# A GCN recommender on one core: the last bias spread by TensorE, two branches turned, constant products between gathers

## The reference

```python
def gcn_conv(x, W, b, src, dst, n):
    h = x @ W
    loops = jnp.arange(n, dtype=src.dtype)
    s, d = jnp.concatenate([src, loops]), jnp.concatenate([dst, loops])
    deg = jax.ops.segment_sum(ones, d, num_segments=n)
    dis = jnp.where(deg > 0, jax.lax.rsqrt(jnp.maximum(deg, 1e-12)), 0.0)
    msgs = h[s] * (dis[s] * dis[d])[:, None]
    return jax.ops.segment_sum(msgs, d, num_segments=n) + b

user_vec = user_emb[user_idx]                                 # 512 x 32
g = jax.nn.relu(gcn_conv(service_emb, W1, b1, src, dst, 6250))
g = gcn_conv(g, W2, b2, src, dst, 6250)
ctx = g[context_idx].reshape(512, 96)
x = jnp.concatenate([user_vec, ctx], axis=1)                  # 512 x 128
return x @ fc_W + fc_b                                        # 512 x 6250
```

## Time and profile before

| | us |
|---|---|
| median of 3 runs | 757.84 |
| their range | 755.71 to 758.91 |
| the profiled execution's own time | 756.2 |
| its span (first to last instruction) | 754.4 |
| TensorE busy | 598.7 (79%) |
| VectorE busy | 599.4 (79%) |
| ScalarE busy | 423.0 (56%) |
| GpSimd busy | 180.4 (24%) |
| granted clock of TensorE, mean | 0.891 of full speed |

### The profile page before, as it was taken

How to read it: one execution, slowest core, us unless ns; L and a number is a source line. 1 busy time by engine, 2 the same in 40 slices (tenths; PEclk the granted TensorE clock), 3 DMA queues, 4 the chain that set the end, 5 groups by cost and what they waited for, 6 DMA issues and landing times.

```text
span 754.4 us, 22006 instructions
## 1 busy us (share of the span) xinstructions
PE 598.7 (79%) x9516; PEld 562.5 (75%) x9516; DVE 599.4 (79%) x1436; ACT 423.0 (56%) x769; POOL 180.4 (24%) x181
## 2 busy tenths in 40 slices
PE   0443657657558665488989999999999999999797
PEld 0343557657558665478989999999999999999443
DVE  9999999999999999888999999999994211111486
ACT  4997089788888511246888888888877100000000
POOL 1100000020000000377777666666200000000600
PEclk9957679699687875588999999999999999999899
DMA  8000000000000000234655565556200799999386
GB/s 130 2 1 1 1 1 1 1 4 3 0 4 2 1 1 1 59 94 136 208 194 192 197 211 205 198 192 211 69 3 2 250 373 359 373 336 289 66 342 284
DMA packets 55337, 94.22 MB, mean 125 GB/s; under 512 B 20954, under 2 KB 42132, under 8 KB 55237
## 3 DMA queue, kind: packets, MB, share of 16 engines
q1 hardware_dynamic: 40532, 74.35, 27.8%
q0 software_dynamic: 5216, 9.91, 6.1%
q10 hardware_dynamic: 9488, 8.52, 3.5%
HBM read 48.53 MB, written 44.21 MB: 123 GB/s over the span
## 4 chain that ended last, share of the span: by engine, by line
PE 49%; DVE 41%; ACT 3%; DMA 2%; issue 2%; POOL 2%; SPq 0%; DVEq 0%; POOLq 0%
PE pp L1482 16%; PE pp L1500 14%; DVE arena L984 13%; DVE arena L985 12%; PE psY L1500 12%; PE pp L1601 6%; DVE arena L971 3%; DVE arena L1162 2%; ACT arena L732 2%; POOL arena L675 1%; PE pp L1418 1%; DMA arena<-ordered_keys,window 1%; DVE arena L979 1%; DVE arena L1149 1%; DVE arena L980 1%
## 5 line engine op out<-in xcount | busy, mean ns | idle before, releaser
L675 POOL DMA_INDIRECT arena<-ordered_keys,window x147 | 159.2, 1083 | 211.6 <-DMA ordered_keys<-arena 147.5
L812 ACT ACTIVATE arena<-pp 128x512 uint16<-128x512 f32 x308 | 171.9, 585 | 47.0 <-PE pp L1482 44.9
L1482 PE MATMUL pp<-arena 128*128 128x128 fp8e4 (+1 forms) x2401 | 188.7, 220 | 7.4 <-DVE arena L1163 7.4
L732 ACT ACTIVATE arena<-arena,neg_word 128x780 fp8e4<-128x780 bf16 (+1 forms) x200 | 170.2, 946 | 0.0
L1482 PEld LDWEIGHTS pp<-arena 128*128 128x128 fp8e4 (+1 forms) x2401 | 147.9, 98 | 8.2 <-issue 5.3
L1500 PE MATMUL psY<-arena 128*128 128x96 bf16 x2401 | 149.9, 206 | 0.5 <-ACT arena L812 0.4
L1500 PEld LDWEIGHTS psY<-arena 128*128 128x128 fp8e4 x2401 | 122.4, 97 | 1.4 <-ACT arena L812 0.7
L1162 DVE TENSOR_SCALAR arena<-arena 128x384 int32<-128x384 int32 (+7 forms) x224 | 110.2, 493 | 7.2 <-PE pp L1482 7.0
L984 DVE TENSOR_TENSOR arena<-arena 128x832 f32<-128x832 f32 (+4 forms) x121 | 107.4, 888 | 3.9 <-ACT arena L755 1.1
L985 DVE TENSOR_TENSOR arena<-arena 128x832 f32<-128x832 f32 (+4 forms) x121 | 106.9, 884 | 0.0
L1500 PE MATMUL pp<-arena 128*128 128x96 bf16 x2401 | 102.4, 206 | 0.6 <-issue 0.6
(11 more groups left out here) (205 smaller groups left out, 520.9 us busy)
## 6 DMA issues: line engine op xcount, KB each, us to landing
arena<-adjacency_spill SPq DMA_DIRECT2D x120, 196.0 KB, 4.1
adjacency_spill<-arena SPq DMA_DIRECT2D x21, 768.0 KB
out_dram<-arena SPq DMA_DIRECT2D x12, 512.0 KB, 2.8
adjacency_spill<-arena SPq DMA_DIRECT2D x7, 832.0 KB
arena<-adjacency_spill SPq DMA_DIRECT2D x22, 197.5 KB, 4.0
out_dram<-arena ACTq DMA_DIRECT2D x8, 512.0 KB, 2.9
arena<-in_L_rec_fc_b_dram SPq DMA_DIRECT2D x7, 392.0 KB, 8.5
adjacency_spill<-arena SPq DMA_DIRECT2D x4, 640.0 KB
```

Source lines behind the costliest of these rows:

```text
L675: nc.gpsimd.indirect_dma_start(gath[:, k, q, :], None, ordered, bass.IndirectOffsetOnAxis(ap=window[:, q, d:d + 1], axis=0)).then_inc(gat[ ...
L732: ins = nc.scalar.activation(cols8[n % BUFS][:, 4 * u:4 * u + 4, 0:c1 - c0], high4[:, :, c0:c1], ACT.Sign, bias=neg_word[:, u:u + 1], satu ...
L812: nc.scalar.mul(adj16[g % SLOTS][:, m0 * P:m1 * P], bank(gp)[:, 0:(m1 - m0) * P], PAIR_SCALE).then_inc(evicted, 1)
L1482: ins = MM(bank(gp)[:, (n - n0) // 2 * P:((n - n0) // 2 + 1) * P], src_hot(h, n - a), dst_hot(h, n - a), start=n % 2 == 0, stop=n % 2 == 1 ...
```

## The change

`fc_b` is no longer spread by the DMA. SyncE loads its 6250 numbers as 13 rows of up to 512 (12x512 and 1x106), three times over, into partitions 0 to 12, 32 to 44 and 64 to 76 of a cleared tile `b_rows`; they lie in space that the one-hot codes no longer need. VectorE does the clearing and then `spread_bias` once, at the end of group 12's turn (`g == NG - 2`): it turns the three copies into the upper, middle and lower bf16 part of the numbers (`b_parts`), and makes 13 matrices `b_pick` of 96x128 that pick one row of each third. After the second layer TensorE multiplies `b_pick[n]` with `b_parts`, thirteen products of 128x512 whose every row is the bias of those 512 columns, and VectorE (even n) and ScalarE (odd n) copy them to SBUF as `fcb`.

The products of constants: 4 in place of 36 behind the second layer, 3 behind the bias, and 4 behind each of the first two gathers of b = 0, which get a semaphore each (`first_rows`).

On VectorE and ScalarE `If(is_bad == 0)` with the usual path first becomes `If(is_bad == 1)` with the general path first. On TensorE and SyncE the order stays.

```diff
--- before.py
+++ after.py
@@ -91,7 +91,8 @@
 FIRST_FETCHES = {3: 3, 4: 16, 5: 28}
 LAG = 3
 SPILL_PARTS = 4
-RUN_UP = (8, 12, 36)
+RUN_UP = (8, 12, 4, 3)
+BETWEEN_ROWS = 4
 AHEAD_OF = {1: 12, 2: 12}
 LOADS_A_CHUNK = 4
 FC_PART = 784
@@ -404,6 +405,12 @@
         featT = at(E0 + 4 * RES_B, BATCH * 4, F32)
         xt = at(E0 + 4 * RES_B + BATCH * 4, 4 * GC * D * 4, F32).rearrange("p (k h f) -> p k h f", k=4, f=D)
 
+        b_rows = at(E0, BANK * 4, F32)
+        b_parts, b_mid = (at(E0 + BANK * 4 + k * BANK * 2, BANK * 2, BF16) for k in range(2))
+        b_of = at(E0 + 2 * BANK * 4, 64, F32)[:, 0:len(NCH)]
+        b_pick = at(E0 + 2 * BANK * 4 + 64, len(NCH) * P * 2, BF16).rearrange("p (n m) -> p n m", m=P)
+        assert 2 * BANK * 4 + 64 + len(NCH) * P * 2 <= 4 * RES_B and len(NCH) <= 32
+
         pp = [ctx.enter_context(nc.psum_tensor(f"pp{k}", [P, 2 * BANK], F32)) for k in range(3)]
         psY = ctx.enter_context(nc.psum_tensor("psY", [P, BANK], F32))
         psX = ctx.enter_context(nc.psum_tensor("psX", [P, BANK], F32))
...
+        first_rows = [sem(f"first_rows{c}") for c in range(CTX)]
+        b_zero, b_in, b_split, b_mm, psum_free = map(sem, ("b_zero", "b_in", "b_split", "b_mm", "psum_free"))
+        b_set = [sem(f"b_set{k}") for k in range(2)]
...
@@ -533,6 +543,8 @@
             w = min(SUBC, T - s * SUBC)
             eng.dma_start(ordered[s * SPAN:s * SPAN + w * P, :].rearrange("(j q t) o -> q j (t o)", q=P, t=P),
                           rows[:, s * SUBC // P:(s * SUBC + w) // P, :]).then_inc(ordered_out[WRITTEN[s]], 16)
+
+        fcW, fcb = (at(adj_at[place2[(NG + k) % 5]], N * 4, F32) for k in range(2))
 
         def write_out(eng, mine):
             out_v = out.rearrange("(p b) n -> p b n", b=BB)
@@ -590,21 +602,22 @@
                     c, e = (min(n * PAIR // 2 * 2 * P, bytes_of(g)) for n in (a, b))
                     sp.wait_ge(evicted, pairs_before(g) + b)
                     sp.dma_start(spill[g, :, c:e], at(adj_at[g % SLOTS] + c, e - c, U8)).then_inc(spilled[g % SLOTS], 16)
+            sp.wait_ge(b_zero, 1)
+            full = N // BANK
+            for k in range(3):
+                sp.dma_start(b_rows[32 * k:32 * k + full, :], fc_b[0:full * BANK].rearrange("(c n) -> c n", n=BANK)).then_inc(b_in, 16)
+                sp.dma_start(b_rows[32 * k + full:32 * k + full + 1, 0:N - full * BANK], fc_b[None, full * BANK:N]).then_inc(b_in, 16)
             for k in range(SLOTS):
                 sp.wait_ge(spilled[k], 16 * SPILL_PARTS * len(range(k, NSPILL, SLOTS)))
             sp.wait_ge(bad_set, 1)
             is_bad = nc.sync.value_load(bad[:], min_val=0, max_val=1)
 
-            def load_fc(slot, what):
+            def load_fc(slot):
                 tile = at(adj_at[slot], N * 4, F32)
-                whole = fc_W if what == 0 else fc_b[None, :].to_broadcast((P, N))
                 for c in range(0, N, FC_PART):
                     w = min(FC_PART, N - c)
-                    if what == 0:
-                        sp.dma_start(tile[0:CTX * D, c:c + w], whole[D:P, c:c + w]).then_inc(fc_in, 16)
-                        sp.dma_start(tile[CTX * D:P, c:c + w], whole[0:D, c:c + w]).then_inc(fc_in, 16)
-                    else:
-                        sp.dma_start(tile[:, c:c + w], whole[:, c:c + w]).then_inc(fc_in, 16)
+                    sp.dma_start(tile[0:CTX * D, c:c + w], fc_W[D:P, c:c + w]).then_inc(fc_in, 16)
+                    sp.dma_start(tile[CTX * D:P, c:c + w], fc_W[0:D, c:c + w]).then_inc(fc_in, 16)
 
             with sp.If(is_bad == 0):
                 sp.wait_ge(filled, pairs_before(NG))
@@ -615,9 +628,8 @@
                     for c in range(0, loads_of(ORDER[i]) * part, part):
                         w = min(part, bytes_of(ORDER[i]) - c)
                         sp.dma_start(at(adj_at[place2[i]] + c, w, U8), spill[ORDER[i], :, c:c + w]).then_inc(loaded[place2[i]], 16)
-                for k in range(2):
-                    sp.wait_ge(y2_done, NG - 4 + k)
-                    load_fc(place2[(NG + k) % 5], k)
+                sp.wait_ge(y2_done, NG - 4)
+                load_fc(place2[NG % 5])
             with sp.Else():
                 sp.wait_ge(g_set, 1)
                 for row, tile in ((1, g_int[0]), (0, g_src)):
...
@@ -694,7 +705,7 @@
             for b in range(BB):
                 for c in range(CTX):
                     nc.gpsimd.indirect_dma_start(feat[:, b, D * c:D * (c + 1)], None, table,
-                        bass.IndirectOffsetOnAxis(ap=ccl[:, b * CTX + c:b * CTX + c + 1], axis=0)).then_inc(rows_in[b], 16)
+                        bass.IndirectOffsetOnAxis(ap=ccl[:, b * CTX + c:b * CTX + c + 1], axis=0)).then_inc(rows_in[b] if b else first_rows[c], 16)
 
         @block.scalar
         def _(act):
@@ -824,10 +835,7 @@
                 c = first_chunk(g)
                 act.dma_start(table[c * P:(c + w) * P, :].rearrange("(h l) f -> l h f", l=P), xt[:, i % 4, 0:w, :]).then_inc(table_out[i % 4], 16)
 
-            with act.If(is_bad == 0):
-                for i, g in enumerate(ORDER):
-                    write_table(i, g)
-            with act.Else():
+            with act.If(is_bad == 1):
                 for layer in range(2):
                     act.wait_ge(g_table, 16 * (layer + 1))
                     with act.Fori(0, TURNS_G) as i:
@@ -835,6 +843,13 @@
                         nc.scalar.copy(g_stage, g_src[:, bass.ds(i * U, U)]).then_inc(g_staged, 1)
                 for g in range(NG):
                     write_table(g, g)
+            with act.Else():
+                for i, g in enumerate(ORDER):
+                    write_table(i, g)
+            for n, (c, w) in enumerate(NCH):
+                if n % 2 == 1:
+                    act.wait_ge(b_mm, n + 1)
+                    nc.scalar.copy(fcb[:, c:c + w], bank(n)[:, 0:w]).then_inc(b_set[1], 1)
             write_out(act, 1)
 
         @block.vector
@@ -1204,6 +1219,18 @@
                 link(V.tensor_reduce(worst[:], flag_row, axis=AX.X, op=ALU.max))
                 V.tensor_scalar(bad[:], worst[:], 0.0, None, ALU.is_gt).then_inc(bad_set, 1)
 
+            def spread_bias():
+                dve.wait_ge(b_in, 96)
+                link(V.tensor_copy(b_parts[:, :], b_rows[:, :]))
+                link(V.tensor_tensor(b_rows[:, :], b_rows[:, :], b_parts[:, :], ALU.subtract))
+                link(V.tensor_copy(b_mid[:, :], b_rows[:, :]))
+                V.tensor_copy(b_parts[32:64, :], b_mid[32:64, :])
+                link(V.tensor_tensor(b_rows[:, :], b_rows[:, :], b_mid[:, :], ALU.subtract))
+                V.tensor_copy(b_parts[64:96, :], b_rows[64:96, :])
+                link(V.tensor_tensor(b_of, ident[:, 0:len(NCH)], ident[:, 32:32 + len(NCH)], ALU.add))
+                link(V.tensor_tensor(b_of, b_of, ident[:, 64:64 + len(NCH)], ALU.add))
+                V.tensor_copy(b_pick[:, :, :], b_of.rearrange("p (n o) -> p n o", o=1).to_broadcast((P, len(NCH), P))).then_inc(b_split, 1)
+
             group_masks(0)
             group_fields(0)
             one_hots(0, 0)
@@ -1256,6 +1283,9 @@
                 if g + 2 < NG:
                     group_fields(g + 2)
                 post_sum(g)
+                if g == NG - 2:
+                    V.memset(b_rows[:, :], 0.0).then_inc(b_zero, 1)
+                    spread_bias()
             post_split(NG - 1)
             is_bad = nc.vector.value_load(bad[:], min_val=0, max_val=1)
 
@@ -1263,17 +1293,7 @@
 
                 V.tensor_tensor(x, x, dis_w(first_chunk(g), chunks_of(g)), ALU.mult).then_inc(table_ready, 1)
 
-            with dve.If(is_bad == 0):
-                for i, g in enumerate(ORDER):
...
-                    to_table(g, x)
-            with dve.Else():
+            with dve.If(is_bad == 1):
                 V.memset(g_zero, 0.0)
...
+            with dve.Else():
+                for i, g in enumerate(ORDER):
...
+                    to_table(g, x)
+
+            V.memset(b_of[:, 0:1], 0.0).then_inc(psum_free, 1)
+            for n, (c, w) in enumerate(NCH):
+                if n % 2 == 0:
+                    dve.wait_ge(b_mm, n + 1)
+                    V.tensor_copy(fcb[:, c:c + w], bank(n)[:, 0:w]).then_inc(b_set[0], 1)
 
             def copy_features(b):
                 dve.wait_ge(feat_T, b + 1)
@@ -1341,7 +1375,8 @@
                 V.tensor_scalar(featT[0:CTX * D, b * P:(b + 1) * P], psX[0:CTX * D, b % 2 * P:(b % 2 + 1) * P], bias2[:, 0:1], None, ALU.add).then_inc(feat_ready, 1)
             copy_features(0)
             mix_features(0)
-            dve.wait_ge(fc_in, 48 * -(-N // FC_PART))
+            for k in range(2):
+                dve.wait_ge(b_set[k], len(range(k, len(NCH), 2)))
             n = 0
             for b in range(BB):
                 for c, w in NCH:
@@ -1574,10 +1609,19 @@
                         ins = MM(ps[k][:, 0:w * D], g_zero[:, 0:P], g_zero[:, 0:w * D], start=False, stop=True)
                     ins.then_inc(g_summed, 1)
 
```

(20 more changed lines are left out.)

18 lines of the change are left out of this document (8 added, 10 removed).

## The result

The changed kernel takes 753.71 us in the median of 20 runs (750.75 to 759.55), the kernel before 757.7 us in 20 runs (754.74 to 761.18). The ratio is 0.995, 95% interval 0.9934 to 0.9966: 3.8 us faster, between 2.6 and 5.0. That is just at the bound of 0.5% that I had set. In two further sets of runs the same code stood at 0.996 (0.9941 to 0.998) and 0.9942 (0.9912 to 0.9973); one execution in the last, of 764.78 us, was in a slower state and stands outside that ratio. The forecast of 752.3 us was right in sign and 1.4 us too low; the range held the time.

The account below looks back on a forecast made before the run. The prediction took the chain through TensorE's second layer, then the last table write, gathers and output products, as the bound. Write -2.7 and clock -2.0 sum to -4.7 us, from 757.0 to 752.3 us; range 750.2 to 756.4.

Parts of the forecast that it names:

- Write of the table: Last write of `context_table`: without the spread load's traffic it takes 2.0 us instead of 4.7, -2.7 us.
- Preparing on VectorE: VectorE's preparing of the bias rows at group 12: at most 13.3 us, covered by idle time of 13.15 us, 0 us.
- Spreading: Thirteen bias products and their copies behind the second layer: done by 698.8, ahead of the transpose at 700.8, 0 us.
- Products by gather: Products of constants between the gathers keep TensorE's clock up for transpose and output and delay nothing: -2.0 us.
- Order of the branches: Jumps of VectorE and ScalarE moved ahead of the second layer: copies start at once, nothing else gained, 0 us.
- my start of 757.0: Whole kernel's starting time for the forecast: the middle of the profiled execution's 756.2 us and the runs' median, 757.84.
- Rival 1: TensorE's clock falls between the gathers, features come 1.2 us late: -2.5 us in all, 754.5 us; chance 0.23.
- Rival 3: Thirteen bias products each wait for a copy, end at 710 and hold the output by 4.6 us: about 761; chance 0.05.

Follow-up runs that it names:

- after: The first profile of the changed kernel, unaltered: the profiled execution took 754.08 us, with a span of 752.3.
- e9: Changed kernel with bias products ahead of TensorE's jump, 12 products of constants behind them, 4 and 1 between the gathers: 754.39 us, ratio 0.994 to the kernel before.
- e10: Changed kernel with only the bias products moved ahead of TensorE's jump, products of constants unaltered: 755.7 us, ratio 0.9956 to the kernel before.
- e11: The changed kernel once more, unaltered, in the last set, as a third profile: 755.44 us, ratio 0.9942 to the kernel before.
- e7: Changed kernel plus the spread load of fc_b as before, into a slot that nobody reads: 757.79 us, ratio 0.9997 to the kernel before.
- e3: Kernel before without the spread load of fc_b, nothing in its place: 756.92 us, ratio 0.9975 to the kernel before.
- e2: Changed kernel with the order of the branches on VectorE and ScalarE as before: 753.78 us, ratio 0.9955 to the kernel before.
- e1: Changed kernel with no products of constants between the gathers: 755.13 us, ratio 0.9967 to the kernel before.
- e6: Changed kernel with 4 products of constants behind the first gather and 1 behind the second: 753.37 us, ratio 0.9949 to the kernel before.
- e5: Changed kernel with TensorE's branch turned too, general path first: 762.79 us, ratio 1.0062 to the kernel before.
- e4: Kernel before with only 4 products of constants added behind each of the first two gathers, spread load kept: 757.3 us, ratio 1.0.

## Why the prediction was right, and where it was not

- *Write of the table, -2.7.* In the profile it is 4.71 to 1.51, -3.2. Over the ten profiles without the traffic it took 1.43 to 3.28 us, 2.4 in the mean (1.51, 2.34 and 2.79 in the changed kernel, mean 2.2), so my 2.0 us was somewhat short, and the profile shown above is a lucky one. What the prediction takes from the Trainium skill there is said, in the section that it names, of transfers that GpSimd issues; this one is issued on ScalarE's queue. The ten fall into two kinds. In three (`after`, `e9`, `e10`) the write landed in 1.43 to 1.51 us, and no packet of an instruction queue was under way while its own 144 packets moved; in the other seven one of q8 (16 KB) or q14 (8 KB) was, and it landed in 2.34 to 3.28 us. From the trace of `e11`, 692 to 694:

```profile
q10 hardware_dynamic: 144, 0.02, 6.2%
q8 instruction: 1, 0.02, 4.1%
```

(q10 is the write.) The three short writes are all in executions whose pause in the second layer was 1.9 us, so what a long pause costs, a short write gives back in part. That the gain depends on the traffic is shown by `e7` (2.8 us lost with it) and `e3` (1.9 us won without it, not clear by itself). How the loss arises in `e7` isn't shown.
- *Preparing on VectorE, 0.* Right: 8.9 us in an idle stretch of 13, 4.31 us left. No wait behind 588.8.
- *Spreading, 0, "cover of 2 us at the dear end".* This is the step that failed in part. Products and copies by themselves are as cheap as reckoned (`e9`: 3.18 us). But TensorE's jump costs a pause of 0.76, 1.64 and 2.16 us in the three profiles of the changed kernel, not at the jump itself but behind the third product, and in `e11` the clock fell in that pause and nearly doubled what was left. I had priced a jump at 1.1 us from the share of queue q8 and called it hidden for the copies. I did not follow it into the clock and the products of constants queued behind: the copies were in time (done by 699.7 to 700.3), TensorE was not.
- *Products by gather, -2.0.* The clock stood at 1.00 through the output in the changed kernel's profiles. The output stage went from 45.55 us (705.37 to 750.92) to 43.84, -1.7; from transpose to first output product from 2.1 to 1.65, -0.5. Together -2.2, for the -2.0 that I took and the -2.4 that I named as the most. But I wrote that the products "delay nothing", since the gathers' landings would be 1.25 us apart like their issues. They aren't: by the landings in the trace of the changed kernel they came at 701.00, 702.29 and 702.46, and 1.16 us of products stood between the second and the transpose. That and the pause make the transpose late in all three of its profiles, by 0.9, 0.6 and 2.3 us behind the third landing; before it was 0.14. This delay, in the mean 1.1 us more than before, is the term that I put at nothing.
- *Order of the branches, 0.* Right in time (`e2`), wrong in the reason: the jump takes 3.0 us, not 1.1, and what hides it seems to be TensorE's own pause.
- *The sum against the profile.* The first profile's -4.6 us behind the last tile, for -4.7 predicted, is luck: a write 0.7 us shorter than the mean of the three, with a late transpose against it. 3.2 us of it were lost again in that execution by a pause and a low clock ahead of the tile, which come and go in executions of every version. Over the three profiles the gain behind the last tile is 4.6, 4.1 and 2.0 us, mean 3.6, and the 20 runs say 3.8. It adds up from the parts: -2.5 for the write, -2.2 for the clock, +1.1 for the late transpose. So what is missing to my -4.7 is mostly that delay; the rest of the 1.4 us is my start of 757.0, where 20 runs say 757.7. There is only one profile of the kernel before to set against them, so this is the likely account and not a proof.
- *Rival 1* (clock falls between the gathers) did occur, but from TensorE's pause in `e1`, `e6`, `e7` and `e11`, or from its wait for VectorE's jump in `e2`, and not from the gaps between the gathers. In `e5` and `e10` it fell among them, after TensorE had stood still for over 3 us until the first gather's products began. *Rival 3* (the output waits for the bias) was right about the place and wrong about the price: in `e6`, `e7` and `e11` the bias products and what is queued behind them hold the transpose by 1.4 to 2.3 us, not the output by 4.6; in the changed kernel's other two profiles they don't.

## What to carry to other kernels

Work put into a covered stretch is only free if each engine is back in time for what is queued behind it; follow the jump, the pause and the clock into the next instruction of the same engine and not only into the result's consumer. Products of constants between arrivals keep the clock up or bring it back, but they count with their full length in front of the work that they wait for, and arrivals are bunched where issues are evenly spaced. A jump should stand where its engine is truly waited for by nobody, and a large broadcast by DMA should not run on the same DMA engines beside a small transfer that everything waits for.

## What the runs showed of the hardware

- A jump over the general path costs 3.02 us on VectorE (`e2`) and 4.8 us on TensorE (`e5`); where TensorE has the jump behind the second layer, 0.76 to 2.46 us of pause appear in six profiles, not at the jump but three products behind it, and they move with the jump (`e9`, 1.77 us, there straight at it).
- TensorE pauses for 0 to 2.41 us at one and the same product of a long unbroken series, in executions of kernels that don't differ up to there. Like the pauses at the jumps, each ends 1.27 to 1.70 us after the end of a 16 KB packet of the instruction queue q8 (22 pauses in 13 profiles). That it is a wait for instructions is inferred from this; why the packet is late is open.
- One of the first three gathers, each of 128 rows, lands 2.27 to 4.02 us (both `e7`) after its issue, the third sooner than the first two in all profiles but one (`e3`), so that they come bunched.
- The 16 KB write of the table takes 4.60 and 4.71 us in the midst of the spread load's traffic (`e4`, before), 1.43 to 1.51 us with that gone and no instruction packet beside it (three profiles), and 2.34 to 3.28 us with one beside it (seven).
